# First tile of a quaternion-like FFN: condition loads on GpSimd's queue, magnitude sums moved to VectorE, down's weights paired before TensorE mixes them

## The reference

```python
W = weights[condition]                       # (32, 64, 64)
y = einsum('bct,bcd->bdt', x, W)             # 2048 rows of 1024
# ternary weights: scale = mean(|W|), Wq = scale * clip(round(W / scale), -1, 1)
# octonion linear: M[k,o,i,d] = sum_j S[j,i,k] * Wq[j,o,d],  out = einsum('...id,koid->...ko', xp, M)
gate = oct_ternary_linear(y, w_gate); up = oct_ternary_linear(y, w_up)   # 8 x 342 hidden columns
h = silu(gate) * up
out = x + oct_ternary_linear(h, w_down)
```

## Time and profile before

| | |
|---|---|
| median of 3 runs | 723.83 us (722.28 to 724.03) |
| the profiled execution, its own time | 724.41 us |
| its span, first to last instruction | 722.6 us |
| mean granted clock of TensorE, share of full | 0.987 |
| busy: PE, DVE, ACT, POOL | 687.3, 538.6, 332.3, 352.5 us |

### The profile page before, as it was taken

One profiled execution on the slowest core, in us unless ns is written; L12 is line 12 of the kernel. 1 busy time (PEld: TensorE's weight loads), 2 busy tenths in 40 slices (PEclk: granted clock), 3 DMA queues, 4 the chain that ended last, 5 costly groups with the idle time before them and its releaser, 6 DMA issues.

```text
span 722.6 us, 17130 instructions
## 1 busy us (share of the span) xinstructions
PE 687.3 (95%) x7046; PEld 625.0 (86%) x7046; DVE 538.6 (75%) x867; ACT 332.3 (46%) x530; POOL 352.5 (49%) x409
## 2 busy tenths in 40 slices
PE   3679998999999999999999999999999999999995
PEld 3468887999999989999899999999899998988895
DVE  1898956767876688676877678766877678777877
ACT  5543485155444546255452555344452554434531
POOL 0200557435736466344856356364753357464553
PEclk9799999999999999999999999999999999999999
DMA  8100003021002110031001110031000300021001
GB/s 327 59 2 1 1 2 122 30 89 64 1 2 88 33 61 2 2 118 63 1 2 52 66 63 2 2 117 62 4 1 11 108 2 1 2 88 31 1 2 59
DMA packets 10576, 31.51 MB, mean 44 GB/s; under 512 B 3330, under 2 KB 3330, under 8 KB 10370
## 3 DMA queue, kind: packets, MB, share of 16 engines
q1 hardware_dynamic: 9906, 28.81, 11.2%
q10 hardware_dynamic: 592, 1.61, 0.7%
HBM read 22.02 MB, written 8.39 MB: 42 GB/s over the span
## 4 chain that ended last, share of the span: by engine, by line
PE 85%; DVE 7%; ACT 3%; issue 2%; POOL 1%; DMA 1%; ACTq 0%; DVEq 0%; POOLq 0%
PE ps L1016 58%; PE ps L1108 21%; PE ps L1003 4%; DMA cond_bd<-in_L_cond_weights_dram 1%; DVE pu_sb L723 1%; ACT down_c L705 1%; POOL z_f L531 1%; PE ps L1010 1%; DVE o_sb L443 1%; ACT z_op L632 1%; DVE ps L843 1%; POOL h_pairs L531 1%; DVE z_op L830 0%; ACT ps L652 0%; DVE gate_table L723 0%
## 5 line engine op out<-in xcount | busy, mean ns | idle before, releaser
L1016 PE MATMUL ps<-y_op,gate_table 128*128 128x256 f16 x2112 | 273.0, 275 | 5.7 <-DVE y_op L816 4.2
L1016 PE MATMUL ps<-y_op,up_table 128*128 128x256 f16 x2112 | 270.7, 273 | 0.2 <-DVE up_table L768 0.2
L1016 PEld LDWEIGHTS ps<-y_op,gate_table 128*128 128x128 f16 x2112 | 207.6, 99 | 30.6 <-DVE y_op L816 4.3
L1016 PEld LDWEIGHTS ps<-y_op,up_table 128*128 128x128 f16 x2112 | 207.1, 98 | 25.1 <-DVE up_table L768 0.7
L531 POOL TENSOR_TENSOR h_pairs<-h_f 128x256 f32<-128x256 f32 (+1 forms) x128 | 121.1, 975 | 151.8 <-ACT h_f L618 94.1
L531 POOL TENSOR_TENSOR z_f<-h_pairs 128x512 f32<-128x512 f32 x80 | 102.7, 1305 | 102.6 <-DVE z_op L830 100.8
L652 ACT ACTIVATE ps<-ps,small 128x512 f32<-128x512 f32 x96 | 63.6, 662 | 175.5 <-DVE ps L843 125.4
L443 POOL TENSOR_TENSOR o_sb<-o_sb,wd_sb 128x256 f32<-128x256 f32 (+1 forms) x150 | 88.3, 626 | 92.7 <-DVE wd_sb L891 91.5
L1108 PE MATMUL ps<-down_c,h_op 128*128 128x128 f16 x1536 | 93.1, 220 | 3.0 <-ACT down_c L705 3.0
L723 DVE TENSOR_TENSOR pu_sb<-ps,q_sb 128x512 f32<-128x512 f32 x96 | 65.8, 686 | 38.7 <-ACT q_sb L646 26.0
L1108 PEld LDWEIGHTS ps<-down_c,h_op 128*128 128x128 f16 x1536 | 89.8, 98 | 4.0 <-ACT down_c L705 3.1
(11 more groups left out here) (75 smaller groups left out, 480.7 us busy)
## 6 DMA issues: line engine op xcount, KB each, us to landing
x_in<-in_x_dram SPq DMA_DIRECT2D x8, 1024.0 KB, 5.3
o_sb<-in_x_dram SPq DMA_DIRECT2D x16, 512.0 KB, 3.6
out_dram<-o_sb SPq DMA_DIRECT2D x15, 512.0 KB, 2.7
h_op<-in_L_ffn_w_gate_dram ACTq DMA_DIRECT2D x3, 512.0 KB, 6.8
h_op<-in_L_ffn_w_up_dram SPq DMA_DIRECT2D x3, 512.0 KB, 7.4
z_op<-in_L_ffn_w_down_dram SPq DMA_DIRECT2D x1, 1536.0 KB, 11.4
out_dram<-o_sb SPq DMA_DIRECT2D x2, 256.0 KB, 2.1
cond_bd<-in_L_cond_weights_dram SPq DMA_DIRECT2D x30, 16.0 KB, 3.0
```

The source lines that it names most:

```text
L1016: mm = pe.matmul(dst, table[m][:, slot, q, :], y_op[:, op, e, :], start=(i == 0 and e == 0), stop=(i == len(terms) - 1 and e == 1))
```

## The change

Four things are changed, all in the preparation of the weights and in the first tile.

1. The four condition transfers of tile 0 are issued by POOL (they count on a semaphore of their own), after its memsets. SP and ACT issue none of them. SP's wait for the index now stands ahead of the conditions of tile 1.
2. DVE sums the magnitudes of windows 0 and 1 of up, ahead of everything else that it does, and ACT only window 2. DVE's order before the first chunk is rearranged: `ternary_of(1, 0)` moves ahead of `y_lo`, and `scales_of_ffn` and `h_scales` go behind it.
3. DVE adds and subtracts down's ternary weights in pairs (`down_pairs`, two additions of 128x512 float16 per window, written where the raw weights stood), and `mix` takes two terms and not four. `z_hi` waits for mixes where it waited for ternary weights.
4. The four rounds of y of tile 1 stand ahead of `own` of the chunks 1, 2, 3 and 4, where they stood behind `own` of 1 and 2 and before and behind `own` of 3. The 16 `down_c` copies come behind the chunks 8, 9 and 10 (6, 5, 5) and not 8 to 11 (4 each).

```diff
-    Y_AT_FIRST = {(1, 1): 0, (2, 1): 1, (3, 0): 2, (3, 1): 3}
+    Y_AT_FIRST = {(1, 0): 0, (2, 0): 1, (3, 0): 2, (4, 0): 3}
-    CORR_AFTER = (8, 9, 10, 11)
+    CORR_AFTER = {8: range(0, 6), 9: range(6, 11), 10: range(11, 16)}
...
+            pool.wait_ge(idx_loaded, 16)
+            pool.wait_ge(cond_zeroed, 1)
+            for b in range(BPT):
+                load_one_cond(pool, 0, b, first_cond_loaded)
...
-                if T == 0 and k % 2 == 0:
+                if T == 0 and k < NQ:
                     for m in range(2):
-                        act.wait_ge(slots_built[m], NBUILD * min(NQ, k + 2))
-                    if k > 0:
-                        act.wait_ge(tern_ready[2], NQ)
+                        act.wait_ge(slots_built[m], NBUILD * (k + 1))
+                elif T == 0:
+                    act.wait_ge(down_mixed, 4 * (k - NQ + 1))
...
-            for w in range(NQ - 1):
-                sum_abs_of(1, w)
+            sum_abs_of(NQ, 1, NQ - 1)
...
+            for w in range(NQ - 1):
+                dve.wait_ge(up_loaded[w], 16)
+                dve.tensor_reduce(abs_sum[1][:, w:w + 1], raw[1][w].rearrange("p j o -> p (j o)"), AX.X, ALU.add,
+                                  apply_absolute_value=True).then_inc(abs_summed_dve, 1)
             scales(0)
             ternary_of(0, 0)
             build_table(0, 0)
             y_scales(0)
-            dve.wait_ge(up_loaded[NQ - 1], 16)
-            dve.tensor_reduce(abs_sum[1][:, NQ - 1:NQ], raw[1][NQ - 1].rearrange("p j o -> p (j o)"), AX.X, ALU.add,
-                              apply_absolute_value=True).then_inc(abs_summed_dve, 1)
             scales(1)
+            ternary_of(1, 0)
+            y_lo(0, range(2))
+            build_table(1, 0)
+            y_lo(0, range(2, NY))
             scales_of_ffn()
             h_scales(0)
-            y_lo(0, range(2))
-            ternary_of(1, 0)
-            build_table(1, 0)
-            y_lo(0, range(2, NY))
             ternary_of(0, 1)
...
                             ternary(2, w, tern_down[:, w], raw_down[w], next(n_tern))
+                            dve.wait_ge(tern_ready[2], w + 1)
+                            t = tern_down[:, w]
+                            for place, sign in ((slice(0, 4), 1), (slice(4, 8), -1)):
+                                signed_add(down_pairs[w][:, place], t[:, 0::2], t[:, 1::2], sign).then_inc(down_paired, 1)
...
-                pe.wait_ge(tern_ready[2], w + 1)
+                pe.wait_ge(down_paired, 2 * (w + 1))
...
-                                       start=(r == 0 and t == 0), stop=(t == 3), skip_group_check=True)
+                                       start=(r == 0 and t == 0), stop=(t == 1), skip_group_check=True)
```

More of the change, by code:

```diff
@@ L261, in build @@
         raw_down = [of_window(raw_down_at, w) for w in range(NQ)]
+        down_pairs = [raw_down_at[:, w * raw_n:w * raw_n + raw_n // 2].bitcast(F16).rearrange("p (j o) -> p j o", j=8)
+                      for w in range(NQ)]
         tern_down_at = o_sb[:].rearrange("p a t -> p (a t)")[:, 0:NQ * raw_n // 2].bitcast(F16)
@@ L425, in build @@
                 for a in range(2):
-                    first = 4 * (h ^ v) + 2 * a
+                    pair = 2 * (h ^ v) + a
                     sign = f[2 * a] * (1, parity(r1))[a]
                     other = parity(r0) if f[2 * a] == f[2 * a + 1] else -parity(r0)
-                    terms += [(first, sign), (first + 1, sign * other)]
-                mixes[h, v, r] = sorted(terms, key=lambda t: -t[1])
+                    terms.append((pair if other > 0 else 4 + pair, sign))
+                mixes[h, v, r] = terms
         MIXES = [(w, h, v) for w in range(NQ) for h, v in F_SIGN]
@@ L458, in load_one_cond @@
             eng.dma_start(cond_bd[C * h:C * h + C, b // 2, C * h:C * h + C],
-                          cond_w[bass.ds(which, 1), :, :].rearrange("a c d -> (a c) d")).then_inc(cond_loaded, 16)
+                          cond_w[bass.ds(which, 1), :, :].rearrange("a c d -> (a c) d")).then_inc(loaded, 16)
         block = ctx.enter_context(nc.Block())
@@ L488, in _ @@
             load_x(0)
-            sp.wait_ge(idx_loaded, 16)
-            sp.wait_ge(cond_zeroed, 1)
-            for b in range(BPT // 2):
-                load_one_cond(sp, 0, b)
             for w in range(NQ):
@@ L672, in sum_abs, with sum_abs_of @@
                 act.activation(junk[:, 0:size], src, ACT.Abs, accum_out=dst).then_inc(abs_summed, 1)
[L674 removed]
+            def sum_abs_of(n, m, w):
                 act.wait_ge((gate_loaded, up_loaded)[m][w], 16)
[L676 removed]
+                sum_abs(n, raw[m][w].rearrange("p j o -> p (j o)"), raw_n, abs_sum[m][:, w:w + 1])
             for w in range(NQ):
                 act.dma_start(raw[0][w], w_gate[:, w]).then_inc(gate_loaded[w], 16)
[L680 to L683 removed]
             act.wait_ge(ones_set, 1)
@@ L702, in _ @@
                         act.wait_ge(tern_ready[2], NQ)
-                        i = per_chunk * CORR_AFTER.index(c)
-                        for (h, v, p), (_, ((j, eight),)) in corr_list[i:i + per_chunk]:
+                        for i in CORR_AFTER[c]:
+                            (h, v, p), (_, ((j, eight),)) = corr_list[i]
                             act.activation(down_c[:, :, v, p, h, :], tern_down[:, :, j, :], ACT.Copy,
```

30 lines of the change are left out of this document (15 added, 15 removed).

## The result

| | before | after |
|---|---|---|
| median, us | 722.88 (722.08 to 724.03, 6 runs) | 727.04 (725.88 to 727.32, 6 runs) |
| profiled execution, us | 724.41 | 727.32 |
| its span, us | 722.6 | 725.6 |
| mean granted clock | 0.987 | 0.985 |
| start of `down` of tile 0, us | 112.56 | 115.64 |

The changed kernel is 0.5% slower: ratio 1.0052, with a 95% interval from 1.0040 to 1.0064. The forecast was 721.3, with a range that ended at 723.6. The profiled span is 3.0 us longer, and all of it has come about by the start of `down` (3.08 us) and of tile 1 (3.07).

The account below looks back on a forecast made before the run. DVE's chain ahead of tile 0's `down` was taken as the bound, the second tile as unchanged. Start 1.9 + rounds of y 3.85 - lowered clock 1.0 - pairs 2.2 = 2.55 us gain: 721.3, range 719.7 to 723.6.

Parts of the forecast that it names:

- What bounds the kernel: Whole kernel: second tile keeps its length, gains only by an earlier tile 0 `down`; DVE hardly idles in chunks 0 to 7.
- The conditions: Start of tile 0: conditions land at some 10 us, scale of gate 0.7 us earlier, within a start gain of 1.9.
- the sum 2.2 + 4.2 + 3.0: Start: index there at 2.2, four issues in 4.2, landing 3.0 us later gives 9.4, taken as some 10.
- POOL issues slowly: Rival, start: POOL's slow issue lands the conditions at 12.5, total gain only 0.35 us, 723.5 us; chance 0.16.
- The rival that the engines are shared: Start: conditions land at 10.9 as before, start gain 1.25, total gain 1.9 us, 721.9 us; chance 0.2.
- The start's order: Start on DVE: up's sum and wait (1.87 us) go; first gate products at 24.5 against 26.2, chunk 0 at 32.6.
- The rounds of y: Chunks 1 to 4: DVE's three waits for PE go, gain 3.85 us, less 1.0 for a lowered clock.
- The pairs: DVE in chunks 0, 6 and 7: six added operations cost 2.2 us, 3.0 as the end.
- Mixing two terms: PE's mixes: 5.4 us less work over 12 mixes, counted as no gain because PE waits longer for `mix_out`.
- The rival of a lowered clock: Chunks 7 to 11: PE's longer waits for `mix_out` lower its clock, a slower kernel at 728.0 us; chance 0.07.
- The copies: Chunks 8 to 11: moved `down_c` copies only shift time between chunks, effect 0.

Follow-up runs that it names:

- e7: Changed kernel with the loads of x, gate, up and down held until the four conditions have landed; 733.08 us, one execution, slower because of the held loads.
- e2: Changed kernel with only the condition transfers put back on SP's and ACT's queues; 725.15 us, ratio 1.0015 to the kernel before.
- e3: Changed kernel without the pair additions, so PE mixes four terms again, conditions still over POOL; 722.81 us, ratio 0.9981 to the kernel before.
- e4: Changed kernel with POOL's first sums of h (first round of z) held until all pair additions are done; 725.49 us, ratio 1.0026 to the kernel before.
- e6: Kernel before with only the four rounds of y of tile 1 moved to chunks 1, 2, 3 and 4; 721.52 us, ratio 0.9971.
- e8: Kernel before with the new rounds of y, all four conditions issued by SP ahead of its windows, x on ACT's queue ahead of gate; 720.86 us, ratio 0.9964.
- e5: Changed kernel with the conditions back on SP and ACT and without pairs; 721.17 us, ratio 0.9962 to the kernel before.
- e1: Kernel before with only the four condition transfers of tile 0 issued by POOL; 725.27 us, ratio 1.0019.

## Why the prediction was wrong, point by point

The change costs 3.08 us up to `down` in the two profiled executions, and I had forecast a gain of 2.55: 5.6 us apart. The start accounts for 3.0 of them, the pairs for 2.3, and the rounds for 0.3 or so, each read from one trace.

**What bounds the kernel: right.** The second tile kept its length (83.50 of 83.50 us busy, 83.60 before), everything was decided by the start of tile 0's `down`, and DVE was the engine that decided it in chunks 0 to 7, but for its waits for PE (0.50 us ahead of chunk 0, 1.3 in the chunks 2 to 4).

**The conditions: wrong, and this step failed first.** The step was the sum 2.2 + 4.2 + 3.0, taken up to 10, for the landing of the last transfer; it landed at 12.3. POOL's issues took the 4.2 us, or a little less (3.69 to 7.67), but began at 3.69 and not at 2.2. And I had a transfer land 3.0 us after its issue, from the earlier trace rows, where it took 5.3. Those 30 are transfers of later tiles. At the start, the two on ACT's queue had taken 6.8 us and the last one 6.52 in my own rows. (The prediction speaks of four on ACT's queue; two of them went over SP's, behind x.) I had put their long transit down to their place behind gate and expected another queue to take it away. It took away a part: 6.7 us became 5.3. e7 shows how much is the traffic: 1.9 us alone, 5.3 beside the loads, in the same queue and at the same issue times.

What I had not asked at all is when the last of four transfers is issued if one engine issues them all: at 7.15, where two engines had been through at 4.40. Against the kernel before, this is the whole reason for the late landing: 2.75 us later at the issue, 1.4 us shorter in transit, 1.3 us later at PE. The rival "POOL issues slowly", to which I gave 0.16, had nearly the right landing (12.5, measured 12.3), though not by its mechanism: POOL issued at SP's pace. The rival that the engines are shared kept the landing of before and missed the later issue as well.

The Trainium skill, page "DMA: Bandwidth & Descriptors", section "Issuing engines are not separate DMA queues", states that transfers from different engines run on the same 16 engines; 5.3 against 1.9 us agrees. The same page of the Trainium skill has the section "Queues, rings and completion order", by which each engine takes turns between its queues by packet; it had made me expect that a third queue passes the loads. It did not pass them freely: 3.4 us of waiting were left for 16 KB.

**The start's order: wrong.** The removed sum and its wait were there (1.87 us), and so was the new order; I had named POOL as a danger for the pairs and had not asked what POOL does at 20 us. It sums y from 19.04 to 24.46 in e2. Before, the magnitude sum (1.14 us on the chain), the wait and the small operations lay beside POOL (20.21 to 23.7); the sum took as long there as without POOL in the changed kernel (1.21 and 1.22 us in the timelines), so DVE lost nothing there; now the ternary weights of up and `y_lo` lie there. They grew by 1.9 us, and POOL's own sums from 4.12 to 5.42. The first gate products came at 28.61, forecast 24.5: of these 4.1 us, 2.3 come with the late scale of gate (16.37, forecast 14.1) and 1.8 with the way from there. Chunk 0 is only 3.0 us later than forecast (35.60, forecast 32.6): from the gate products to it I had 8.1 us, as before, and it took 6.99, most of it because the clock was back earlier. That part is luck of this execution; in e3 it took 8.38.

The Trainium skill, page "SBUF — State Buffer", section "Who interferes with whom", describes one port pair that VectorE and GpSimd share as an exclusive lock, where the other one blocks until the instruction ends. The rows agree in that both engines grew longer when they ran beside each other (1.28 to 1.63 and 2.17, 0.75 to 1.84, 4.12 to 5.42), and that DVE's are back when POOL waits (e4). The same section of the Trainium skill names an operation with two SBUF inputs; the one-input form (0.75 to 1.84) is hit as well, and whether by the fast mode that the section also names, no run here shows.

**The rounds of y: right in the main, the gain mis-sized by 0.8.** Forecast were a PE wait of 2.5 us in chunk 1 (measured 2.40), a lowered clock behind it, and 3.85 - 1.0 = 2.85 us net. The chunks 1 to 3 gain 2.53 us together, and e6 alone 0.0029 of the time, 2.1 us by the ratio. The 3.85 counted all three waits of DVE for PE, and the last of them, 0.81 us in chunk 4, stayed in every run. It is not the lowered clock's: it is there in e8, too, where the clock did not fall and PE had no gap. I had PE reach the end of that chunk's products 0.1 us ahead of DVE's want; it is 0.8 behind. Without the fall, chunks 1 to 3 gain 3.18 us (e8); with it 2.53 in the changed kernel and 1.52 in e6. So the fall cost 0.65 and 1.66 us, around the 1.0 of the sum and up to the 1.65 that it had as an end. It is the one part that works.

**The pairs: mis-sized.** The term was 2.2 us, with 3.0 as its end; measured were 0.79, 1.74 and 1.94, so 4.5. An addition takes 0.38 us where POOL is quiet, near the 0.34 of the sum. For the additions beside POOL I took an extra of 0.15, with 0.95 as its end (2.17 and 1.29 differ by 0.88); two of them lie there, in chunk 6, and it is 0.94. The end was reached by one pair of additions, and I had used it for all. Those of chunk 7 take 0.76, since POOL is through at 88.35. What I had not counted is in chunk 7 all the same: the additions of chunk 6 push its ternary weights to another place of POOL's work, and L749 grows from 0.75 to 1.59. The cost of an inserted operation beside another engine is its own stretching and that of what it shifts. The 0.33 us for silu are left without a cause: they come with the pairs (e4 has them, e3 not), and ACT was idle before that silu. No run tells more.

**Mixing two terms: right at nothing.** PE's work fell by 4.5 us, its waits for `mix_out` grew from 1.0 to 8.6 us, and no chunk got shorter. The rival of a lowered clock came true in its first half: PEclk was 0.57 from 86 to 90 us, behind a wait of 2.75 us. It passed nothing on, because PE's products had slack there. Its time (728.0) is near the measured 727.04 by chance; e3 and e4 put the cost in DVE's rows.

**The copies: right at nothing.** Chunks 8 to 10 are 0.77, 0.41 and 0.41 longer, the end 1.59 shorter, which sums to zero; e5 against e6 says the same.

By differences of the ratios: conditions over POOL +0.0019 (e1), pairs +0.0053 (e2 against e5), rounds of y -0.0029 (e6), start and copies -0.0009 (e5 against e6, not told from zero). Their sum is +0.0034, or 2.5 us, against +0.0052 measured in six runs beside a median that lay low by up to 1.2 us (0.0017).

## What to carry to other kernels

A landing time is the moment of the last issue plus a transit, and the transit is read from the traffic that the transfer will meet: 16 KB took 1.9 us in empty DMA engines and 5.3 beside full ones. Another queue shortened the last transit by 1.4 us here, and the head of a queue by 2.8, but one issuer for all four instead of two issued the last one 2.75 and 2.3 us later. Before work is moved on VectorE, or an operation inserted, look at what GpSimd does at the new times, for the inserted operation and for all that it shifts; a gap in VectorE that lay beside GpSimd's work had kept the two apart, and filling it cost the 1.9 us that it gave. And a shorter piece of work on the engine that waits was worth nothing here, so the price of shortening it on the engine that doesn't wait is the whole balance.

## What the runs showed of the hardware

- Two additions of 128x512 in float16 on DVE took 0.76 us alone and 1.70 beside POOL's float32 sums; 128x1024 of float32 to float16 took 0.75 alone and 1.09, 1.35 (e3), 1.59 and 1.84 beside them; POOL's five additions went from 4.12 to 5.42 us. Both sides can lose: in the kernel before, the same operation kept its 0.75 us at 84.19 us, and POOL's two sums took 3.04 instead of 2.48.
- PE's waits of 2.2 to 2.4 us were followed by a lowered clock (0.50 to 0.57 over 2 to 4 us) in some executions and not in others, with the same wait and the same instructions (before against e1 at 51 us; e6 against e8 at 37 us). So was the wait of 2.97 to 2.98 us ahead of `down` (lowered before, in e1 and e8; at 1.00 in e6), and the clock after the wait of about 7 us at the start came back 2 to 3 us sooner or later (the changed kernel against e3). A fall cost 1.67 us of a chunk, and the kernel's runs lie in two groups 1.7 us apart (medians of 722.44 and 724.15 in the first batch). That is as much as a part of this change is worth, so a few runs of each kernel don't tell such a part from the clock.
- POOL issued a transfer with a computed address each 1.15 us, 0.52 of it the issue itself; SP took 1.05 to 1.07 (4.20 and 4.27 us for four).
- A transfer of 16 KB landed 1.9 us after its issue with no loads beside it (e7, GpSimd's queue), and beside the loads after 5.3 (GpSimd's queue), 4.9 (first on SP's, e8) and 6.7 us (behind x and gate on SP's and ACT's, before).
